# Patch tokens, linear attention and a top-2 mixture of experts on one core: the last steps of the token stage reordered, and the weights' left-over parts made per tile

## What is computed

```python
concat = [x, four copies shifted by 4 pixels]              # 10 channels
h = conv8x8(layernorm(concat) * gamma + beta) + b           # 169 tokens of 128 per image
y = layernorm(h)
q, k, v = heads(y @ Wqkv.T)                                 # 8 heads of 64
q1, k1 = exp(q * 64**-0.5 @ proj.T), exp(k @ proj.T)
o = (q1 @ (k1.T @ v)) / (q1 @ sum(k1) + 1e-6)
h = h + o @ Wout.T + bout
z = layernorm(h)
g = z @ Wg                                                  # 8 experts, top 2, softmax over the two
h = h + sum over the 2 chosen e: gw[e] * (silu(z @ W[e]) * (z @ V[e])) @ W2[e]    # 128 -> 512 -> 128
```

## Time and profile before

| what | value |
|---|---|
| median of 3 runs (lowest, highest) | 1203.25 us (1201.57, 1204.62) |
| profiled execution, its own time | 1201.72 us |
| its span | 1199.9 us |
| mean granted TensorE clock | 0.97 of 2.4 GHz |
| busy share of the span: TensorE, VectorE, POOL, ScalarE | 91%, 72%, 50%, 47% |
| token stage up to the last h2 product | 0 to 703 us |
| expert stage from its first hidden product | 732 to 1200 us |

### The profile page before, as it was taken

One profiled execution on the slowest core, in us unless ns is written; L12 is line 12 of the kernel. 1 busy time (PEld: TensorE's weight loads), 2 busy tenths in 40 slices (PEclk: granted clock), 3 DMA queues, 4 the chain that ended last, 5 costly groups with the idle time before them and its releaser, 6 DMA issues.

```text
span 1199.9 us, 30227 instructions
## 1 busy us (share of the span) xinstructions
PE 1095.0 (91%) x8632; PEld 926.2 (77%) x8633; DVE 858.7 (72%) x3327; ACT 567.8 (47%) x1318; POOL 605.2 (50%) x666
## 2 busy tenths in 40 slices
PE   2699999999999999999999726999999999999994
PEld 1567777777777777776766525999999999999994
DVE  4448787887787878878867584777777777777772
ACT  2343634535445354353333414555555555555551
POOL 2001535354445354444445452676666666666664
PEclk9799999999999999999999857999999999999997
DMA  9251131220301312101011143343444443444442
GB/s 155 49 140 60 34 73 33 47 60 27 80 26 36 72 34 63 44 30 33 27 33 32 34 119 63 54 55 53 55 53 54 56 55 53 54 54 53 57 54 21
DMA packets 75792, 65.54 MB, mean 55 GB/s; under 512 B 12382, under 2 KB 66718, under 8 KB 75712
## 3 DMA queue, kind: packets, MB, share of 16 engines
q0 software_dynamic: 33024, 25.86, 15.3%
q1 hardware_dynamic: 42496, 38.32, 13.7%
q10 hardware_dynamic: 192, 0.37, 0.2%
HBM read 32.81 MB, written 31.71 MB: 54 GB/s over the span
## 4 chain that ended last, share of the span: by engine, by line
PE 68%; issue 13%; DVE 7%; POOL 2%; SPq 1%; DMA 1%; ACT 1%; POOLq 0%; DVEq 0%; ACTq 0%
PE bank L1251 22%; PE bank L1263 13%; PE bank L581 7%; PE bank L653 4%; PE bank L640 3%; PE bank L646 3%; PE bank L535 3%; PE bank L627 2%; DVE patches L745 2%; DVE xtok L855 2%; PE bank L425 2%; DVE attn L794 2%; POOL rstd L1130 2%; PE bank L1239 2%; PE bank L628 2%
## 5 line engine op out<-in xcount | busy, mean ns | idle before, releaser
L1392 POOL DMA_INDIRECT out_rows<-yo,dest x184 | 302.2, 1643 | 168.8 <-issue 116.4
L1251 PE MATMUL bank<-xT_e,wv 128*128 128x256 f32 x2208 | 289.1, 286 | 1.0 <-DVE xT_e L1343 0.9
L1251 PEld LDWEIGHTS bank<-xT_e,wv 128*128 128x128 f32 x2208 | 271.9, 190 | 1.6 <-DVE xT_e L1343 1.3
L1155 POOL DMA_INDIRECT sorted_rows<-xrow_all,sloti x192 | 189.0, 984 | 74.7 <-issue 54.4
L1321 ACT ACTIVATE sil<-bank 128x256 f32<-128x256 f32 x368 | 141.5, 385 | 160.1 <-PE bank L1251 157.2
L1350 DVE TENSOR_TENSOR hid<-sil,bank 128x256 f32<-128x256 f32 x368 | 154.7, 421 | 84.2 <-ACT sil L1321 74.3
L1263 PE MATMUL bank<-w,hid 128*128 x1472 | 179.5, 275 | 1.0 <-DVE hid L1350 1.0
L1263 PEld LDWEIGHTS bank<-w,hid 128*128 128x128 f32 x1472 | 171.5, 192 | 1.2 <-issue 1.2
L1128 POOL TENSOR_SCALAR vare<-mv 128x3 f32<-128x3 f32 x64 | 12.5, 196 | 310.4 <-issue 255.0
L1306 ACT CAST wv<-wv_all 128x1024 fp32r x92 | 96.3, 1047 | 40.9 <-issue 27.9
L1066 ACT ACTIVATE attn<-bank 128x256 f32<-128x256 f32 x128 | 49.5, 387 | 131.1 <-PE bank L629 131.1
(11 more groups left out here) (188 smaller groups left out, 1856.8 us busy)
## 6 DMA issues: line engine op xcount, KB each, us to landing
xr<-sorted_rows SPq DMA_DIRECT2D x92, 130.0 KB
raw<-in_x SPq DMA_DIRECT2D x64, 84.5 KB
raw<-in_x SPq DMA_DIRECT2D x60, 78.0 KB
out_rows<-attn SPq DMA_DIRECT2D x64, 58.5 KB
sorted_rows<-xrow_all,sloti POOLq DMA_INDIRECT x192, 2.3
out_rows<-yo,dest POOLq DMA_INDIRECT x184
wv_all<-in_L_ffn_W SPq DMA_DIRECT2D x8, 256.0 KB, 6.4
wv_all<-in_L_ffn_V SPq DMA_DIRECT2D x8, 256.0 KB, 6.7
```

What stands on the lines that cost most here:

```text
L1155: po.indirect_dma_start(sorted_rows, bass.IndirectOffsetOnAxis(sloti[:, p, j, ch:ch + 1], 0), xrow[:, p, j, ch], None).then_inc(s(f"scatte ...
L1251: q = pe.matmul(bank[fc][:, TT * m:TT * m + TT], wv[:, p, w_, m, cols], xT[:, p, x_], start=(w_ + x_ == 0), stop=(w_ == 1))
L1392: po.indirect_dma_start(out, bass.IndirectOffsetOnAxis(dest[:, p, a:a + 1], 0), yo[:, p, a], None, compute_op=ALU.add).then_inc(s(f"added{ ...
```

## The change

In the token stage:
- SP loads the down weights at step 32, ahead of that step's stores. The pads at the ends of the lists go half to SP, half to ScalarE's queue. SP reads the row numbers of tiles 0 and 1 ahead of its waits for pads and scatters.
- The pieces `lo_high` and `lo_low` and the tensor `wl_all` are gone.
- VectorE: in the last steps the denominators come ahead of the normalised rows; `choose` moves from behind the last normalisation to behind the normalised rows in step 32, and to the head of steps 33 and 34.
- TensorE: the ranks' products of the last steps move ahead of the attention output; in steps 33 and 34 ahead of the broadcasts.
- POOL: 3 chunks of scatters ahead of the root in step 32, 2 in step 33, 1 as before in step 31.
- ScalarE: after the last step a Silu of a small tensor, then its four pads.

In the expert stage: `wv` has four buffers instead of two, weights are made two tiles ahead, `low_w` is a subtraction that waits for `high_w` of its tile, and the loops' bodies have four tiles instead of two.

On SP:

```diff
             def step(n, k, g, par, a, b, c, d, fr):
...
+                if n == NPAIR:
+                    sp.wait_ge(s("conv_done"), NPAIR)
+                    for e in range(E):
+                        expert_sync(sp, "down_weights", e)
...
-            sp.wait_ge(s("conv_done"), NPAIR)
-            for e in range(E):
-                expert_sync(sp, "down_weights", e)
-
             sp.wait_ge(s("ends_ready"), 1)
-            for e in range(E):
-                r = sp.value_load(ends[0:1, e:e + 1], min_val=e * CAP, max_val=e * CAP + NTOK)
-                sp.dma_start(sorted_rows[bass.ds(r, TT)].rearrange("(a p) n -> p a n", a=2), pad).then_inc(s("pads_out"), 16)
+            pad_ends(sp, range(0, E, 2))
             for q in range(2):
                 sp.wait_ge(s(f"h2_out{q}"), NPAIR // 2 * 16 * len(PLACES))
+            sp.wait_ge(s("table_ready"), 2)
+            first = [expert_sync(sp, "row_number", t) for t in range(2)]
             sp.wait_ge(s("pads_out"), 16 * (1 + E))
             for q in range(2):
                 sp.wait_ge(s(f"scattered{q}"), NPAIR // 2 * 96)
-            sp.wait_ge(s("table_ready"), 2)
-            expert_sync(sp, "rows", 0)
+            expert_sync(sp, "rows", first)
```

On TensorE:

```diff
                 front(0)
+                if d and not a and not b:
+                    rank()
                 if c:
                     pe.wait_ge(s("rden_ready"), mc + 1)
                     broadcast(0)
...
+                if b and d and not a:
+                    rank()
                 if b:
                     pe.wait_ge(s("x_ones"), mb + 1)
...
-                    if d and i == 1:
-                        pe.wait_ge(s("before_step"), NCH * (md + 1))
...
+                    if a and d and i == 1:
+                        rank()
```

On VectorE:

```diff
-                if not a:
-                    lo_low(ve, n - NPAIR, 0)
-                if d:
+                def normal_rows():
                     ve.wait_ge(s("ln2_rstd"), md + 1)
...
+                if d and a:
+                    normal_rows()
+                if n > NPAIR:
+                    choose(md)
                 if c:
                     ve.wait_ge(s("d8_done"), mc + 1)
...
+                if d and not a:
+                    normal_rows()
+                if n == NPAIR:
+                    choose(md)
...
-                if not a:
-                    lo_low(ve, n - NPAIR, 1)
...
-                if d:
+                if d and a:
                     choose(md)
...
-                if not a:
-                    lo_low(ve, n - NPAIR, 2)
```

On ScalarE, and below it on POOL:

```diff
             steps(ac, step)
+            ac.wait_ge(s("egap_ready"), NPAIR)
+            ac.activation(esum_silu[:], egap[:], ACT.Silu)
+            ac.wait_ge(s("ends_ready"), 1)
+            pad_ends(ac, range(1, E, 2))
             expert_scalar(ac)
...
+                before_root = {NPAIR: 3, NPAIR + 1: 2}.get(n, 1)
...
-                    scatter((0,))
+                    scatter(range(before_root))
...
-                    scatter((1, 2))
+                    scatter(range(before_root, NCH))
```

In the expert stage:

```diff
-    wv = sb("wv", [128, 2, 2, 2, F], F32R)
-    wl_all = sb("wl_all", [128, E, 2, F])
+    wv = sb("wv", [128, 4, 2, 2, F], F32R)
...
-        def low_w(t, p):
+        def low_w(t, w):
             e = expert_of(ve, t)
-            at_least(ve, s("hv_done"), 4 * (t - 1))
-            ve.tensor_copy(wv[:, p, 1].rearrange("p m n -> p (m n)"),
-                           wl_all[:, bass.ds(e, 1)].rearrange("p e m n -> p (e m n)")).then_inc(s("w_low"), 1)
+            ve.wait_ge(s("w_high"), t + 1)
+            at_least(ve, s("hv_done"), 4 * (t - 3))
+            ve.tensor_tensor(wv[:, w, 1].rearrange("p m n -> p (m n)"),
+                             wv_all[:, bass.ds(e, 1)].rearrange("p e m n -> p (e m n)"),
+                             wv[:, w, 0].rearrange("p m n -> p (m n)").bitcast(F32), ALU.subtract).then_inc(s("w_low"), 1)
```

More of the change, by code:

```diff
@@ L204, in tokens @@
         esum = sb("esum", [128, NCH])
+        esum_silu = sb("esum_silu", [128, NCH])
         pick = sb("pick", [128, 2, NCH, E])
@@ L334, in load_edges, with pad_ends @@
                 eng.dma_start(raw44[p0:R1:NP2, :, k0:k0 + HALF], imgs[:, :, y0:y0 + HALF]).then_inc(s("raw_in"), 16)
+        pad = K("padrow").rearrange("p (a n) -> p a n", a=2)
+        def pad_ends(eng, of_experts):
+            for e in of_experts:
+                r = eng.value_load(ends[0:1, e:e + 1], min_val=e * CAP, max_val=e * CAP + NTOK)
+                eng.dma_start(sorted_rows[bass.ds(r, TT)].rearrange("(a p) n -> p a n", a=2), pad).then_inc(s("pads_out"), 16)
         @block.sync
@@ L507, in q_feature, with rank @@
                              lambda a_: xT[:, pb, a_, 0:QW]).then_inc(s("q_mm"), 1)
+                def rank():
+                    pe.wait_ge(s("before_step"), NCH * (md + 1))
+                    if a:
+                        pe.wait_ge(s("ln1_x"), n + 1)
+                    else:
+                        pe.wait_ge(s("h2_copied"), n - 2)
+                        pe.wait_ge(s("logit_read"), n - 2)
+                    pe.matmul(ranks[:, :], ones, before[:].rearrange("p c e -> p (c e)"), start=True, stop=False)
+                    pe.matmul(ranks[:, 0:NCH * E], tri, both[:].rearrange("p c e -> p (c e)"), start=False, stop=True
+                              ).then_inc(s("rank_done"), 1)
                 if n == 1:
@@ L1203, in run @@
         def run(eng):
[L1204 to L1210, removed]
+            step(0, 0, 0, 0, True, False, True)
+            step(1, 0, 1, 1, True, True, True)
+            with eng.Fori(0, (NT - 4) // 4) as i:
+                for u in range(4):
+                    step(4 * i + 2 + u, 2 * i + 1 + u // 2, u % 2, (2 + u) % 4, True, True, True)
+            step(NT - 2, NT // 2 - 1, 0, (NT - 2) % 4, True, True, False)
+            step(NT - 1, NT // 2 - 1, 1, (NT - 1) % 4, False, True, False)
         return run
@@ L1219, in sync, with row_number, rows @@
             return
-        def rows(t, h, p):
-            r = sp.value_load(table[0:1, bass.ds(t, 1), 0], min_val=0, max_val=E * CAP)
+        def row_number(t):
+            return sp.value_load(table[0:1, bass.ds(t, 1), 0], min_val=0, max_val=E * CAP)
+        if what == "row_number":
+            return row_number(e)
+        def rows(t, h, p, r=None):
+            if r is None:
+                r = row_number(t)
             at_least(sp, s("tok_t"), t - 1)
@@ L1226, in rows @@
                          ).then_inc(s(f"rows_in{p}"), 16)
-        rows(0, 0, 0)
-        rows(1, 0, 1)
+        rows(0, 0, 0, e[0])
+        rows(1, 0, 1, e[1])
         with sp.Fori(0, (NT - 2) // 2) as i:
@@ L1240, in turn, with hidden @@
             q.then_inc(s("tok_t"), 1)
-        def hidden(t, p, fc):
+        def hidden(t, p, w, fc):
             if fc == 0:
@@ L1265, in down, with step @@
             q.then_inc(s("y_done"), 1)
-        def step(t, h, p, more, prev):
-            hidden(t, p, 0)
-            hidden(t, p, 1)
+        def step(t, h, p, w, more, prev, more2):
+            hidden(t, p, w, 0)
+            hidden(t, p, w, 1)
             if more:
@@ L1273, in step @@
                 down(t - 1, 1 - p, expert_of(pe, t - 1))
-            hidden(t, p, 2)
-            hidden(t, p, 3)
+            hidden(t, p, w, 2)
+            hidden(t, p, w, 3)
         pe.wait_ge(s("table_ready"), 2)
@@ L1280, in tensor, with high_w @@
         down(NT - 1, 1, expert_of(pe, NT - 1))
[L1283 to L1300 removed]
     def scalar(ac):
[L1303 removed]
+        def high_w(t, w):
             e = expert_of(ac, t)
[L1305 to L1306 removed]
+            at_least(ac, s("hv_done"), 4 * (t - 3))
+            ac.copy(wv[:, w, 0].rearrange("p m n -> p (m n)"),
                     wv_all[:, bass.ds(e, 1)].rearrange("p e m n -> p (e m n)")).then_inc(s("w_high"), 1)
@@ L1323, in scalar @@
         ac.wait_ge(s("table_ready"), 2)
-        ac.wait_ge(s("lo_split"), 2 * E)
+        ac.wait_ge(s("weights_in"), 16 * 2 * E)
+        ac.wait_ge(s("conv_done"), NPAIR)
         high_w(0, 0)
+        high_w(1, 1)
         copy_x(0, 0, 0)
@@ L1365, in step @@
                 low_x(t + 1, 1 - p)
-                low_w(t + 1, 1 - p)
+                if more2:
+                    low_w(t + 2, (w + 2) % 4)
             if prev:
@@ L1374, in vector @@
         ve.wait_ge(s("table_ready"), 3)
-        ve.wait_ge(s("lo_split"), 2 * E)
+        ve.wait_ge(s("weights_in"), 16 * 2 * E)
         low_w(0, 0)
+        low_w(1, 1)
         meta(0, 0, 0)
```

33 lines of the change are left out of this document (5 added, 28 removed).

## The result

The changed kernel takes 1209.8 us in the median of 6 runs (1207.1 to 1210.4), the kernel before 1201.8 beside it; the ratio is 1.006, 95% interval 1.0048 to 1.0072. I forecast 1194.9 and a range up to 1200.5. It is slower by 8 us where I expected 8 us less. Of my steps the transition and the tail came about in kind; the loss in the expert stage was more than three times mine.

What follows compares the result with a forecast made beforehand. TensorE was taken to bound the expert stage, SP's issuing the transition before it. Transition -14.6, left-over weights +5.3 and tail +1.0 made -8.3 from 1201.7: 1193.4, or 1194.9 us as median of runs; range 1187.5 to 1200.5.

Steps and rivals of the forecast that it cites:

- the transition: Last token steps up to the first expert rows: rows requested 14.6 us earlier, bounds 13.1 to 16.2.
- the tail: End of the kernel: the last used tile's add starts 0.98 us later, passed on to the end, +1.0 us.
- the left-over weights' term: Expert stage: the longer, waiting subtraction makes the down products' load 0.12 us late, 0.06 us per tile, 5.3 us in all.
- The rival that VectorE's loop becomes the bound: Expert stage: VectorE bounds every tile, slower than before from 5.03 us a tile, a subtraction of 1.26; 1220 us; chance 6%.
- Four buffers and rounding two tiles ahead gain nothing here: Expert stage: TensorE waits for no weight today, so no gain; they only keep the longer subtraction from being needed at once.
- With 2.4 us to land (3.3 at most, as the adds of the tail): End of the transition: the last scatter lands 2.4 us after its issue, 3.3 at most.
- the pads as a rival for being last: End of the transition: ScalarE's pads issued slowly, pads or scatters landing 2.6 to 4 us later; about 1198.5 us; chance 13%.
- loads and SP's issuing would leave the chain: Before the expert stage: SP's issuing, down-weight loads included, no longer last; a scatter's landing stands there instead.
- pads are covered by about 1 us: End of the transition: pads land at 710 to 713.4 us, ahead of the scatters by about 1 us only.
- the Silu table load costs nothing on the way: ScalarE, after the last step: the 1.28 us table load was covered before and costs nothing in either place.
- the 3.3 forecast: Step 32: attention output starts 3.3 us earlier, the middle between TensorE at 2.4 GHz and at 1.2 GHz.
- my half-clock end: Step 32: attention output starts at 674.8 us if TensorE runs at 1.2 GHz, 673.2 at 2.4 GHz, 677.34 before.

Runs made afterwards that it cites:

- e3: Changed kernel with the subtraction's two waits swapped, the one for the products first, the one for the rounding last: 1206.0 us, ratio 1.004.
- e1: Changed kernel with the subtraction replaced by a copy of the whole weights without the wait for the rounding (output not right): 1189.4 us, ratio 0.9902.
- e4: Changed kernel with two weight buffers, weights made one tile ahead and loop bodies of two tiles, subtraction still behind the rounding: 1238.2 us, ratio 1.0304.
- e2: Changed kernel with VectorE's subtraction one tile behind ScalarE's rounding, so that it never waits for it: 1193.4 us, ratio 0.9935.
- e14: Kernel of e2 with all eight pads on SP again, run beside e13: 1195.6 us, ratio 0.9940.
- e13: Kernel of e2 run again unchanged, as base for later runs: 1192.5 us, ratio 0.9922.
- e15: Kernel of e2 with the down weights' loads behind the last stores on SP again, run beside e13: 1194.4 us, ratio 0.9942.

## Why the prediction was wrong

- **The step that failed** is the left-over weights' term, "0.12 late", halved to 0.06 us a tile and 5.3 us. The mechanism was right, the loop is the one of the chain above, and the length of the subtraction (1.14) too. What was mis-sized is the lateness: 0.26 and 0.51 us by turns instead of 0.12, 0.385 on average. The halving holds: late and nearly punctual tiles alternate (4.93 and 5.09, 4.93 and 5.34), and half of 0.385 is the 0.19 us a tile, 17.7 us, that the run lost.
- Its cause is the price of the handovers. I had put each at 0.04 us, the distance at which a product starts on VectorE behind a Silu (904.62 + 0.38 to 905.04 in the trace before). They measured 0.14 to 0.24 us to the subtraction, 0.13 to the down products' load, and up to 0.13 more on ScalarE. I had allowed 0 to 0.10 us a tile for them all. Standing idle isn't what makes the difference: VectorE was idle for 0.38 us in front of that product as well. In the same trace, every other tile's first product starts 0.12 behind its Silu (909.50 + 0.39 to 910.01). What differs is what an engine still has to do between the wait and the work. e3 shows this for one wait, 0.1 us; for the other handovers I infer it.
- The rival that VectorE's loop becomes the bound is what happened, but not by its price (a subtraction stretched to 1.26 us or more, which it never was). I gave it 6%. Its deciding point was 5.03 us a tile; with the transition and tail as they came out (11.6 less 0.75) it lies at 5.00 by my estimate. At 5.07 the kernel is slower, and e3 is at 5.05.
- "Four buffers and rounding two tiles ahead gain nothing here ... they only keep the longer subtraction from being needed at once": both shown, the first by e1 (4.878 us a tile with four buffers, as before with two), the second by e4. The loop bodies of four tiles cost nothing by themselves (e1). That together with the waits they make one tile in four the longest is read from the 0.81 and 0.24 us in that tile; no run has four buffers and a body of two.
- **Transition**, 14.6 us, bounds 13.1 to 16.2: 11.6 by the marks of the profiled executions, 11.8 with the tail by e1. The last scatters start at 703.34, inside my 702.9 to 705.1. What failed is "With 2.4 us to land (3.3 at most, as the adds of the tail)": 5.17. I had the pads as a rival for being last, not as what slows the scatter. The earlier trace rows ends at 720 us and takes its median over 29 scatters, most of them without pads beside them. For the last six of the kernel before, in 714 to 730 us, the same view has twice that:

```profile
sorted_rows<-xrow_all,sloti POOLq DMA_INDIRECT x6, 5.0
```

- The pads take longer, too: SP's last one is issued at 707.55 and takes 7.0 us to land, where I had 4.1. It lands less than 1 us ahead of the last scatter, so a faster scatter alone would have gained less than that.
- **Tail**, +1.0: measured +0.75.
- That loads and SP's issuing would leave the chain, that pads are covered by about 1 us, and that the Silu table load costs nothing on the way: as read. The attention output of step 32 started at 672.58, 10.3 us behind the sums; before it was 13.7 behind them. The 3.4 us gained are the 3.3 forecast, but with luck: in e2 and e14, where the clock came back later, the output starts 12.0 and 12.4 us behind the sums, beyond my half-clock end (11.2).
- In this trace the clock fell behind the shorter idle stretch: TensorE stood idle for 2.07 us, and the mean granted clock in 667 to 672 us is 0.69. TensorE: Matmul & The Clock Gate (the Trainium skill, Part 1: The HAM clock gate) has the clock follow how busy TensorE has lately been, which I had taken to speak for the full clock.

## What to carry to other kernels

Price a handover by what stands between the wait and the work: take it from a row with the same instructions behind the wait, not from the shortest one (0.04 us here, against 0.12 to 0.24 elsewhere). Where an engine's slack is 0.1 us a tile and several handovers lie on the loop, treat the loop as the bound. Before lengthening an operation inside such a loop, take its wait out of the loop by working one stage behind; length or wait alone cost 0.01 us a tile here, both together 0.19. And for a landing time take the stretch that has the same traffic beside it.

## What I had not expected of the hardware

In step 32, behind 2.0 to 2.1 us without work, TensorE's clock fell in the traces of the changed kernel, e1 to e4 and e13 to e15. It came back at different times, though TensorE has the same work there. Below are two stretches of e13, then the same of e14; the granted clock is the third number from the end, 1.00 for 2.4 GHz and 0.50 for 1.2:

```profile
667.00:672.00 5.00, 4.51 (x17) 3.29 (x16) 4.31 (x20) 1.49 (x3) 2.67 (x6) 0.67 1.01 298
672.00:677.00 5.00, 5.00 (x26) 3.28 (x25) 2.29 (x12) 0.39 (x2) 1.96 (x2) 1.00 0.63 170
```

```profile
667.00:672.00 5.00, 4.16 (x11) 2.97 (x12) 4.40 (x21) 1.19 (x2) 2.90 (x6) 0.56 1.00 278
672.00:677.00 5.00, 5.00 (x16) 3.78 (x15) 1.82 (x11) 0.69 (x2) 1.00 (x1) 0.50 0.68 182
```

In e13 the chip is back at 2.4 GHz by 672, in e14 it stays at 1.2 until past 677, and step 32 is 3.3 us longer. The lengths of the step fall into three groups: 18.6 us in the changed kernel, e1 and e13, 20.3 in e2 to e4, 21.9 in e14 and e15. e2 and e13 are one kernel and lie in two of them, so the difference is not the edit's; what decides it was not tested. It is as large as the parts of the transition that I tried to measure by totals.
